# Last layer's probabilities turned in 32 by 32 blocks on VectorE and through device memory

## The reference

```python
q = (x @ wq.T + bq).reshape(b, n, H, HD).transpose(0, 2, 1, 3)     # k, v in the same way
scores = jnp.einsum('bhnd,bhmd->bhnm', q, k) / jnp.sqrt(jnp.float32(HD))
scores = jnp.where(adj[None, None] == 0, -jnp.inf, scores)
attn = jnp.nan_to_num(jax.nn.softmax(scores, axis=-1), nan=0.0)
out = jnp.einsum('bhnm,bhmd->bhnd', attn, v)
out = out.transpose(0, 2, 1, 3).reshape(b, n, D_OUT)
return out @ wo.T + bo
```

## Time and profile before

| | us |
|---|---|
| median of 3 runs (3006.74 to 3022.74) | 3012.59 |
| the profiled execution | 3014.59 |
| its span in the trace | 3012.8 |

### The profile page before, as it was taken

How to read it: one execution, slowest core, us unless ns; L and a number is a source line. 1 busy time by engine, 2 the same in 40 slices (tenths; PEclk the granted TensorE clock), 3 DMA queues, 4 the chain that set the end, 5 groups by cost and what they waited for, 6 DMA issues and landing times.

```text
span 3012.8 us, 62503 instructions
## 1 busy us (share of the span) xinstructions
PE 2812.3 (93%) x23496; PEld 2665.5 (88%) x23496; DVE 2116.2 (70%) x5995; ACT 2101.1 (70%) x5057; POOL 1501.1 (50%) x2119
## 2 busy tenths in 40 slices
PE   4689999999999999999999999999999999999886
PEld 3689999999999999999999999999999999998874
DVE  3357777777777777777777777777777777777664
ACT  1367777777777777777777777777777777776663
POOL 0245555555555554555555555555555545554442
PEclk8899999999999999999999999999999999999997
DMA  3000000000000000000000000000000000000000
GB/s 106 22 15 19 15 19 22 22 15 19 22 15 19 22 15 22 19 22 15 19 22 15 19 22 21 16 19 22 16 18 22 15 22 19 22 15 8 8 8 11
DMA packets 40606, 60.98 MB, mean 20 GB/s; under 512 B 4592, under 2 KB 21360, under 8 KB 40304
## 3 DMA queue, kind: packets, MB, share of 16 engines
...
...
## 4 chain that ended last, share of the span: by engine, by line
PE 84%; DVE 11%; ACT 2%; issue 1%; POOL 1%; SPq 0%; DMA 0%; POOLq 0%; DVEq 0%; ACTq 0%
PE ps L197 41%; PE ps L213 8%; PE ps L206 6%; PE ps L351 6%; PE ps L310 6%; PE ps L311 6%; PE ps L434 4%; DVE xn L944 3%; PE ps L219 2%; PE ps L333 2%; PE ps L409 2%; DVE act L782 2%; DVE o3Tp_lo L675 1%; DVE pfc L817 1%; DVE act L787 1%
## 5 line engine op out<-in xcount | busy, mean ns | idle before, releaser
L963 POOL TENSOR_TENSOR o1Tp_lo<-o1T,o1Tp_hi 128x1024 fp32r<-128x1024 f32 x64 | 162.0, 2531 | 441.1 <-ACT o1Tp_hi L450 441.1
L915 DVE CUSTOM_DVE_ANT_0 p<-ps,mask 128x256 f32<-128x256 f32 x512 | 194.4, 418 | 143.2 <-PE ps L409 143.2
L1032 POOL TENSOR_TENSOR rd<-some,den 128x2 f32<-128x2 f32 x256 | 87.2, 340 | 395.9 <-DVE den L922 395.7
L1038 POOL TENSOR_TENSOR p<-p,rd 128x512 f32<-128x512 f32 x256 | 267.1, 1043 | 15.6
L648 ACT ACTIVATE p<-p,nmx 128x256 f32<-128x256 f32 x512 | 255.0, 505 | 10.2 <-DVE nmx L915 10.2
L717 DVE CUSTOM_DVE_ANT_0 sco<-ps,mask 128x256 f32<-128x256 f32 x384 | 145.8, 417 | 134.8 <-ACT ps L453 134.8
L450 ACT ACTIVATE xnT_hi<-ps 128x512 fp32r<-128x512 f32 x192 | 115.7, 603 | 178.4 <-PE ps L213 178.4
L975 POOL TENSOR_SCALAR xn<-act,nmean,rstd 128x256 f32<-128x256 f32 x384 | 210.7, 558 | 29.6 <-POOL rstd L970 22.4
L213 PE MATMUL ps<-ident,sco 128*128 128x128 f32 x768 | 123.4, 284 | 75.9 <-ACT sco L458 75.6
L458 ACT ACTIVATE sco<-sco,nmax 128x256 f32<-128x256 f32 x384 | 191.3, 517 | 3.6 <-DVE nmax L717 3.6
L675 DVE TENSOR_TENSOR xnT_lo<-ps,xnT_hi 128x512 fp32r<-128x512 f32 x192 | 130.6, 680 | 81.7 <-ACT xnT_hi L450 81.5
...
## 6 DMA issues: line engine op xcount, KB each, us to landing
x0T<-in_xT SPq DMA_DIRECT2D x64, 256.0 KB, 3.0
x<-in_x SPq DMA_DIRECT2D x64, 256.0 KB, 2.7
out<-xn SPq DMA_DIRECT2D x64, 256.0 KB, 2.2
o1T<-in_mlp SPq DMA_DIRECT2D x1, 512.0 KB, 4.7
p<-in_mlp SPq DMA_DIRECT2D x1, 512.0 KB, 4.6
att<-in_fc SPq DMA_DIRECT2D x1, 512.0 KB, 5.3
ex<-in_fc SPq DMA_DIRECT2D x1, 512.0 KB, 6.3
xn<-in_fc_T SPq DMA_DIRECT2D x2, 256.0 KB, 6.5
```

Of the source, the lines that this page charges most:

```text
L915: ins = V.tensor_tensor_reduce(p4[:, h % 2, m, :], bank[7 - h % 2][:, m, :], mask3[:, m, :], -1.0, BIG, ALU.add, ALU.min, nmx4[:, h, m:m + 1])
L1038: G.tensor_tensor(p4[:, h % 2, :, :], p4[:, h % 2, :, :], rd4[:, h, :].unsqueeze(2).broadcast_to([P, NT, N]), ALU.mult).then_inc(S["p4n"], 1)
```

## The change

- `t40` to `t43` are gone on PE and ACT. In their place DVE has `x40` and `x42`: one instruction each turns the probabilities of a pair of heads (128 by 1024) in place, in blocks of 32 by 32. What such blocks leave undone, moving the blocks to their rows of the 128 partitions, is done by DMAs.
- SP sends the turned pair to a scratch in device memory (`o40`, `o42`: 512 KB each) and loads it from there to `p4T` (`i40`, `i42`: four DMAs of 128 KB each, one for each quarter of the partitions, in pieces of 1 KB).
- `p4` becomes two tiles, one for each pair, so that `s42` writes another tile than `s40`. Their rows are laid out in four groups of 64 columns for each head and row tile: the scores' moving operand `kT` is read in runs of 32 columns (`by_quads`), the mask is made in this order once, and DVE, ACT and POOL write or read p in four runs of 64.
- `s42` (PE) now waits for DVE's reading of heads 0 and 1 (`nmx4`). `a4` waits for `nmx4` of all heads and, before each half, for the four loads of its pair. DVE's steps `s40` to `s43` wait for the scratch to hold the pair of the graph before.
- The orders of all five engines are new. The last layer's latest stage on PE is 9 instead of 7, and the first layer's earliest 2 instead of 0.

```diff
-    "sp": "st:9 lx:1 lt:0",
+    "sp": "lt:0 o40:7 st:9 o42:7 lx:1 i40:7 i42:7",
...
+            def turn_out(c):
+                def step(t):
+                    sp.wait_ge(S["p4x"], 2 * t + c + 1)
+                    wait(sp, p4Tin[c], 16 * QUADS * t)
+                    sp.dma_start(scratch[c], p4[c][:, :, :]).then_inc(p4out[c], 16)
+                return step
+
+            def turn_in(c):
+                def step(t):
+                    sp.wait_ge(p4out[c], 16 * (t + 1))
+                    wait(sp, S["av4_mm"], t)
+                    for w in range(QUADS):
+                        sp.dma_start(p4T[w * QP:(w + 1) * QP, c, :, :], scratch[c][:, w, :].rearrange("(q j) n -> j q n", q=QUADS)).then_inc(p4Tin[c], 16)
+                return step
...
-                            ins = nc.tensor.matmul(bank[7 - g % 2][:, m, :], qT[a][rows_, g // 2, m * P:(m + 1) * P], kT[b][rows_, g // 2, :],
+                            ins = nc.tensor.matmul(bank[7 - g % 2][:, m, :], qT[a][rows_, g // 2, m * P:(m + 1) * P], by_quads(kT[b][rows_, g // 2, :]),
...
             def s42(t):
-                pe.wait_ge(S["p4T"], HEADS * t + 2)
+                pe.wait_ge(S["nmx4"], HEADS * t + 2)
                 scores(2)
 
-            def t4(h):
-                def step(t):
-                    pe.wait_ge(S["p4n"], HEADS * t + h + 1)
-                    transposes(bank[7 - h % 2], p4[:, h % 2, :, :]).then_inc(S["p4T_mm"], 1)
-                return step
-
             def a4(t):
-                pe.wait_ge(S["p4T"], HEADS * t + HEADS)
+                pe.wait_ge(S["nmx4"], HEADS * t + HEADS)
                 for c in range(CT):
+                    pe.wait_ge(p4Tin[c], 16 * QUADS * (t + 1))
                     for k in range(NT):
                         for g in range(2):
                             h = 2 * c + g
-                            ins = nc.tensor.matmul(bank[6][g * HD:(g + 1) * HD, c, :], v4[:, k, h * HD:(h + 1) * HD], p4T[:, h, k, :],
+                            ins = nc.tensor.matmul(bank[6][g * HD:(g + 1) * HD, c, :], v4[:, k, h * HD:(h + 1) * HD], p4Tv[:, c, g, k, :, :, :],
...
-            def t4(h):
-                def step(t):
-                    ac.wait_ge(S["p4T_mm"], HEADS * t + h + 1)
-                    copy(p4T[:, h, :, :], bank[7 - h % 2]).then_inc(S["p4T"], 1)
-                return step
...
+            def turn4(c):
+                def step(t):
+                    dv.wait_ge(S["p4n"], HEADS * t + 2 * c + 2)
+                    V.transpose(p4[c][:, :, :], p4[c][:, :, :]).then_inc(S["p4x"], 1)
+                return step
```

More of the change, by code:

```diff
@@ L46, in graph_stack @@
     HD = C // HEADS
+    QUADS = 4
+    QP = P // QUADS
     MASK = -(2.0 ** 100)
@@ L122, in graph_stack @@
         nmx4 = sb("nmx4", [P, HEADS, NT])
-        p4 = sb("p4", [P, 2, NT, N])
-        p4T = sb("p4T", [P, HEADS, NT, N])
+        p4 = [sb(f"p4_{i}", [P, QUADS, 2 * NT * CT * P // QUADS]) for i in range(2)]
+        p4T = sb("p4T", [P, 2, QUADS, 2 * NT * CT * P // QUADS])
+        p4v = [p4[i][:, :, :].rearrange("p w (g a b j) -> p g a w b j", g=2, a=NT, b=CT) for i in range(2)]
+        p4Tv = p4T[:, :, :, :].rearrange("p c q (g a b i) -> p c g b a q i", g=2, a=NT, b=NT)
         den4 = sb("den4", [P, HEADS, NT])
@@ L131, in graph_stack @@
         STAGED = ("W1T", "W2T", "W_T", "hand_T")
-        W.update({n: p4T[:, i, :, :] for i, n in enumerate(STAGED)})
-        W.update({"mlp2": p4[:, :, :, :].rearrange("p a b n -> p (a b) n"), "mlp1": o1T[0][:, :, :].rearrange("p (a b) n -> p a (b n)", a=2),
+        p4T_flat = p4T[:, :, :, :].rearrange("p c q n -> p (c q n)").rearrange("p (h t n) -> p h t n", h=HEADS, t=CT)
+        W.update({n: p4T_flat[:, i, :, :] for i, n in enumerate(STAGED)})
+        W.update({"mlp2": p4[0][:, :, :], "mlp1": o1T[0][:, :, :].rearrange("p (a b) n -> p a (b n)", a=2),
                   "wqT": sco[0][:, :, :], "wkT": sco[1][:, :, :], "wvT": sco[2][:, :, :], "W3": act[0][:, :, :],
@@ L148, in graph_stack, with by_quads @@
  o3_mm o3T o3Th o3Tl h3_mm h3h h3 f3_mm raw2 nmax2 pro2 rden2 proT2_mm proT2h proT2 av3_mm act2 cut3 ex3 cl3 q3 on3_mm r3 y2 mv2 rstd2 xn2 xnT2_mm xnT2h xnT2
- q4_mm qTh qT k4_mm kTh kT v4_mm v4 sc4_mm nmx4 p4 rd4a rd4 p4n p4T_mm p4T av4_mm o4Th o4T xb4 y4_mm y3 mv3 rstd3 xn3 stored0 stored1""".split()
+ q4_mm qTh qT k4_mm kTh kT v4_mm v4 sc4_mm nmx4 p4 rd4a rd4 p4n p4x p4out0 p4out1 p4T0 p4T1 av4_mm o4Th o4T xb4 y4_mm y3 mv3 rstd3 xn3 stored0 stored1""".split()
         S = {n: ctx.enter_context(nc.semaphore("s_" + n)) for n in names}
         stored = [S["stored0"], S["stored1"]]
+        p4out, p4Tin = [S["p4out0"], S["p4out1"]], [S["p4T0"], S["p4T1"]]
         block = ctx.enter_context(nc.Block())
+        def by_quads(row):
+            return row.rearrange("p (b w j) -> p w b j", b=CT, w=QUADS)
         def wait(eng, sem, n):
@@ L156, in wait @@
                 eng.wait_ge(sem, n)
+        scratch = [nc.dram_tensor(f"scratch{c}", [P, QUADS, 2 * NT * CT * P // QUADS], fp32, kind="Internal").ap() for c in range(2)]
         n_loads = len(weights) - 2 + 2 + HT + 2
@@ L182, in store @@
                 sp.dma_start(out[t].rearrange("(t p) c -> p t c", p=P), xn3[t % 2][:, :, :]).then_inc(stored[t % 2], 16)
-            run("sp", {"lt": load_x0T, "lx": load_x0, "st": store}, B)
+            def turn_out(c):
[11 more added lines that the diff above has]
+                return step
+            run("sp", {"lt": load_x0T, "lx": load_x0, "st": store, "o40": turn_out(0), "i40": turn_in(0), "o42": turn_out(1), "i42": turn_in(1)}, B)
             sp.wait_ge(stored[0], 16 * ((B + 1) // 2))
@@ L678, in _ @@
             V.tensor_scalar(mask16[:, :, :], adj_sb, 0.0, MASK, ALU.is_le, ALU.mult)
-            V.tensor_scalar(mask3[:, :, :], adj_sb, 0.0, MASK, ALU.is_equal, ALU.mult).then_inc(S["setup_dve"], 1)
+            for m in range(NT):
+                ins = V.tensor_scalar(mask3[:, m, :].rearrange("p (w b j) -> p w b j", w=QUADS, b=CT), by_quads(adj_sb[:, m, :]), 0.0, MASK, ALU.is_equal, ALU.mult)
+            ins.then_inc(S["setup_dve"], 1)
             dv.wait_ge(S["setup_dve"], 1)
@@ L913, in step @@
                     dv.wait_ge(S["sc4_mm"], HEADS // 2 * t + h // 2 + 1)
+                    wait(dv, p4out[h // 2], 16 * t)
                     for m in range(NT):
-                        ins = V.tensor_tensor_reduce(p4[:, h % 2, m, :], bank[7 - h % 2][:, m, :], mask3[:, m, :], -1.0, BIG, ALU.add, ALU.min, nmx4[:, h, m:m + 1])
+                        ins = V.tensor_tensor_reduce(p4v[h // 2][:, h % 2, m, :, :, :].rearrange("p w b j -> p w (b j)"), bank[7 - h % 2][:, m, :].rearrange("p (w n) -> p w n", w=QUADS),
+                                                     mask3[:, m, :].rearrange("p (w n) -> p w n", w=QUADS),
+                                                     -1.0, BIG, ALU.add, ALU.min, nmx4[:, h, m:m + 1])
                     ins.then_inc(S["nmx4"], 1)
```

13 lines of the change are left out of this document (7 added, 6 removed), and 8 rows, old and new, of the table ORDERS.

## The result

| | before | after |
|---|---|---|
| median us (4 runs each, side by side) | 3015.49 | 2918.3 |
| lowest to highest | 3006.74 to 3022.74 | 2917.64 to 2920.4 |
| the profiled execution | 3014.59 | 2918.28 |
| its span | 3012.8 | 2916.5 |

What follows compares the result with a forecast made beforehand. TensorE was taken to bound the kernel, busy 42.92 of each 44.18 us period. Removing the transposes saves 112.6 us and all other terms count 0: 3014.6 - 112.6 = 2902 us, range 2870 to 2930.

Steps and rivals of the forecast that it cites:

- the old idle time: TensorE's waits in the loop, 1.26 us a period, mostly for a graph layer's exponentials; forecast to stay.
- the list: TensorE's busy work in one period, forecast to fall from 42.92 to 41.16 us.
- transposes out: Four groups of transposes of p leave TensorE, 0.44 us each: 1.76 us per graph, 112.6 us over 64 graphs.
- the trip: Second pair's way through turn, scratch and loads to a4: there at 15.85 us, 0.75 before its use, costing nothing.
- the walk: Step-by-step layout of the new orders from the end of s42, with a4's second half starting at 16.6 us.
- rival 4: TensorE's old idle time goes too, 0.4 us a period left instead of 1.26: 2847 us, chance 0.10.
- The last leg of the trip: The second pair's four loads from scratch to p4T: issues, then 2.7 us to land, at 15.85; upper bound 4.2.
- the turn: VectorE's block transpose of a pair, 128 x 1024, two a graph: 1.1 us each, far bound 2.4.
- the far end: Latest landing of the second pair's loads by the walk's bounds: 18.95 us, 2.4 late for a4.
- Rival 1: The trip is late by part of the gain: a4 waits 0.3 to 1.2 us a period, 2950 us, chance 0.20.
- rival 3: The trip pays crowded prices, 4.6 us out and 4.2 in: slower, 3149 us at worst, chance 0.14.
- The ends: Fill and drain of the run: forecast as 0, with 5 us either way.

Runs made afterwards that it cites:

- e1: The kernel before, old orders kept, without the transposes of p and their copies, nobody filling p4T: 2946.73 us, 0.9778 of before.
- e2: The changed kernel without the loads from the scratch; the product reads a p4T that nobody fills: 2799.85 us, 0.9294 of before.
- e9: The changed kernel with the last product cut in two, the second pair's half behind r2, and y4 behind m3 and n3: 2883.56 us.
- e10: The changed kernel with the product in two, x and x0T loaded before the second out transfer, and quarters loaded 0, 2, 1, 3: 2866.07 us.

## Why the prediction held, and where it did not

The time, 2918 us, lies in the range, 16 us above the forecast of 2902, and on its side. That it comes so near is luck: the sum left out a gain of 1.64 us a period (the old idle time, and 0.38 in the list) and a cost of 1.89, and these cancel but for 0.25. In periods:

| step | forecast us | measured us | shown by |
|---|---|---|---|
| transposes out | -1.76 | -1.02 by themselves, in the old orders | e1 |
| the old idle time | 1.26 kept | 0 left without the loads | e2 |
| the list | 41.16 | 40.78 | e2 |
| the trip | 0 | +1.89 | after against e2 |
| period | 42.42 | 42.67 | |

**The list and the transposes: right in kind, mis-sized.** 1.76 us is what the chain's pieces hold, and `t40` gave its 0.43; in the old orders 0.74 of the sum did not reach the period, 0.44 of that because TensorE then waited longer for the exponentials, and 0.27 because `m2` waited for VectorE. The forecast read "anything taken from TensorE's list shortens the period, as long as no other engine becomes late for it", and in the old orders one was late already, the one of the earlier trace rows, and another was just in time. The list was taken as 42.92 - 1.76, but 42.92 held two waits' tails beside work; without any wait it is 40.78. That account fits by size: 0.16 us for each of two waits, and 0.09 at `m2`, whose 12 matmuls take 1.61 us from start to start in before where `n2`'s, of the same kind and also behind transposes, take 1.52. It was not tested by itself.

**The idle time kept: failed.** "I leave the idle time of a period at 1.26 us and claim no gain from it" was the cautious choice, although the walk had found no counterpart to the wait. e2 shows that the walk was right: 1400.00 us busy in 1400. The mechanism of rival 4 happened, and in full.

**The last leg of the trip, put at no cost: failed.** Counted from the end of `s42` (1522.13 in the chain's first period), the second turn ends at 8.9 (forecast 8.65), and the second pair is outside at 12.1 (11.7). Up to here every price holds within 0.5 us: the turn at a pitch of 1.16 us (1.1), GpSimd at 1.05 (1.04), the out transfer at 2.9 (3.0). The last load lands at 18.8, not 15.85. The forecast used 2.7 us, the landing of 256 KB of x in a queue with a share of 0.06; the last load took 4.25 and 5.0 (4.2 on average over 32 periods) in a queue that the burst had filled, 32 partitions at a time. That is 0.15 us short of the far end, 18.95, named in the prediction. The value was taken "near the loop's own transfers, since the share of the queue there is 0.06": this share was that of the loop before, and the change puts 2 MB a period into it. Rival 1's mechanism happened, larger than its 0.3 to 1.2 us. The trip's landing price was rival 3's (4.2 us); that rival went too far in the out transfer (4.6, measured 2.9) and in letting the first pair's bytes stand in front of the second's as well.

**The turn and the ports.** The turn takes 1.16 us in the chain. The Trainium skill (VectorE: DVE Perf Modes, The three transpose paths) has 311 ns for a 128x128 bf16 transpose; the prediction's scaling of it to 2.5 us does not hold for this one. The Trainium skill (Vector Engine (DVE) Microarchitecture Reference, The reshape front-end and per-opcode configuration) has "one element per cycle per lane"; the estimate from it, near 1.1 us, agrees with the 1.16. The estimate made from the Trainium skill (SBUF — State Buffer, Door 1: The DMA port swizzle), 2.8 us instead of 1.5 for a pair's loads and some 20 us of the run, was right in direction and too small: against 128 partitions the loads cost 1.16 us a period, 71 us by the medians, because they stood last on the path. The 20 us are also too little by the prediction's own numbers: 1.3 us later with 0.75 to spare is 0.55 a period, 35 us.

**The rest: right.** The scores' matmuls still start 0.12 us apart (0.91 us for a group of 12) and the product takes 1.88 us in e2 as in before, so runs of 32 columns cost nothing. `s42`, `c2`, `n2` and `t0` have no row of waits in after, with their 0.3 to 0.5 us of slack. The walk on TensorE from the end of `s42` to `a4` is 15.84 us in e2, forecast 15.6.

**The ends: right in the sum only.** The last product of the first graph starts at 258.5 us instead of 243.5. Without the loads it starts at 256.5 (e2), so 13 of the 15 us are its place in the new orders and not the trip. By the loop's 1.51 us a period these 15 us and more are won back: at the 55th graph the changed kernel is 68 us ahead. From there to the last graph's product, while the run drains, it gains another 29 us, 15 more than 9 x 1.51. So the fill costs 15 us and the drain gives 15, each outside the 5 us of the forecast, and they cancel by luck. What makes the drain shorter was not followed.

Open remain what makes the groups longer where the product is cut in two (0.3 us a period in e9 and e10), and the shorter drain.
